# Loading the first expert tile's rows by a transfer of its own in a four-stage transformer kernel

## The chip, the cores and the metric

The kernel runs on one core of one Trainium2 chip. The metric is the device time of one execution in microseconds (us), start to end, as the median of the runs. A lower number is better.

## What is computed

Two transformer-like layers work on 2048 tokens (8 sequences of 256) with 256 features. Each layer normalises its input, and adds an attention part and a feed-forward part to it. The change lies in the feed-forward part of the first layer, a mixture of eight experts of which each token uses two, beside a shared expert:

```python
def _mlp(x, gw, uw, dw):
    return jax.nn.silu(x @ gw.T) * (x @ uw.T) @ dw.T
...
topk_idx, topk_w = _route(x2d, router_weight, e_score_correction_bias)
cw = jnp.zeros((T, E), jnp.float32).at[jnp.arange(T)[:, None], topk_idx].add(topk_w)

def expert_body(acc, ws):
    gw, uw, dw, cwe = ws
    y = _mlp(x2d, gw, uw, dw)
    return (acc + cwe[:, None] * y, None)
...
out = routed.reshape(orig_shape) + _mlp(x, shared_gate_w, shared_up_w, shared_down_w)
```

The attention of the first layer is a delta-rule recurrence of 16 heads, the second layer has a test-time-training attention and a second mixture of experts. The change touches none of these three.

## The kernel before

**Order of the stages.** The engines (PE for matmuls, DVE, ACT, POOL, and SP, which issues nearly all transfers) each run a hand-written program; semaphores tie them together. First come the layer norm, the routing and the shared expert, then 39 tiles of the routed experts, then the first attention in a loop over heads, then the second layer.

**The routed experts.** Token rows are sorted by expert through memory. The DRAM tensor `slot_rows` has 39 tiles of 128 rows, each row 256 features, one routing weight and padding, 272 numbers or 1088 bytes in all. SP first fills it with zeros (line 476), counted on the semaphore `e_zero`, which POOL awaits (line 2690) before its own sends. POOL then scatters the tokens' rows into it with 32 indirect transfers (`send`, line 2687), counted on `e_first` and `e_second`. SP waits for all of these (lines 519 and 520), and then loads the tiles back in groups of TG = 3 with `load_tiles` (line 510 on, the transfer on line 513) into `xs`, which has XBUF = 3 group buffers, each with a semaphore of its own, `e_x[g]`. The first three groups are loaded at once, one transfer behind the other; each of the ten later ones is loaded when the group three before it is used up. `store_tiles` (line 515) writes the results of a group to `slot_out`, from where POOL gathers them.

**What PE does per tile.** For each tile `n` the loop at lines 786 to 800 calls, in this order, `turn_x(n)` (line 731: two transposes, line 738), a load of the tile's expert number into a register of PE's sequencer (line 789), `expert_up` of the tile before (line 746), `turn_h` of the tile before that (line 755) and `expert_down` of the tile three back (line 765). `turn_x(n)` waits for `e_x` of its group where `n` is the first of a group. ACT copies each turned tile out (line 1475). Directly before the tiles PE runs the shared expert's last down projection (`shared_down`, line 708), and it then waits for the expert numbers and weights (lines 728 and 729).

The wait and the load, as they stand:

```python
if j % TG == 0:
    pe.wait_ge(e_x[g % XBUF], 16 * (g // XBUF + 1))
```

Of the kernel before, what the change touches and what calls it, by code (L numbers as in the profile page):

```python
# [16 lines left out]
P = 128  # L17
# [24 lines left out]
TG, XBUF, YBUF, GBUF = 3, 3, 2, 3  # L42
# [41 lines left out]
def build(nc, a, out):  # L84
    with ExitStack() as ctx:
# [3 lines left out]
        def sem(name):  # L89
            return ctx.enter_context(nc.semaphore(name))  # L90
# [59 lines left out]
        rt = sem("small_steps")  # L150
        moe_w, e_w = sem("shared_weights"), sem("expert_weights")
        m_gate, m_up, m_silu, m_h, m_down, m_added = (sem("shared_" + n) for n in "gate up silu h down added".split())
        e_zero, e_slots, e_ids, e_first, e_sent, e_second = (sem("e_" + n) for n in "zeroed slots tile_experts first_sent first_weights_gone second_sent".split())
        e_x = [sem(f"e_rows{g}") for g in range(XBUF)]
        e_xt, e_xk, e_gu, e_sg, e_h, e_ht, e_hk, e_dn, e_y = (sem("e_" + n) for n in "x_turned x_kept gate_up silu h h_turned h_kept down y".split())
        e_stored = [sem(f"e_stored{g}") for g in range(YBUF)]
# [7 lines left out]
        def esb(name, shape, dt=F32):  # L164
            return ectx.enter_context(nc.sbuf_tensor(name, shape, dt))
# [25 lines left out]
        xs = esb("xs", [P, XBUF, TG, ROW])  # L191
# [7 lines left out]
        slot_rows = nc.dram_tensor("slot_rows", (TILES0 * P, ROW), F32, kind="Internal").ap()  # L199
# [4 lines left out]
        def asb(name, shape, dt=F32):  # L204
            return actx.enter_context(nc.sbuf_tensor(name, shape, dt))
# [42 lines left out]
        slots = asb("slots", [P, NT, TOP0], mybir.dt.int32)  # L248
# [209 lines left out]
        def _(sp):  # L458
# [51 lines left out]
            def load_tiles(g):  # L510
                if g >= XBUF:
                    sp.wait_ge(e_y, TG * (g - XBUF + 1))
                sp.dma_start(xs[:, g % XBUF], slot_rows[g * TG * P:(g + 1) * TG * P].rearrange("(t p) n -> p t n", p=P)).then_inc(e_x[g % XBUF], 16)

            def store_tiles(g):
                sp.wait_ge(e_y, TG * (g + 1))
# [4 lines left out]
            for g in range(XBUF):  # L521
                load_tiles(g)
            for g in range(GROUPS):
                store_tiles(g)
                if g + XBUF < GROUPS:
                    load_tiles(g + XBUF)
# [53 lines left out]
        def _(pe):  # L580
# [149 lines left out]

            def turn_x(j):
                g = j // TG
                if j % TG == 0:
                    pe.wait_ge(e_x[g % XBUF], 16 * (g // XBUF + 1))
                if j >= 2:
                    pe.wait_ge(e_xk, j - 1)
                for kk in range(KD):
                    last = pe.transpose(bank[1 - j % 2][:, kk * P:(kk + 1) * P], xs[:, g % XBUF, j % TG, kk * P:(kk + 1) * P], ident[:])
                last.then_inc(e_xt, 1)
# [46 lines left out]
            for n in range(TILES0 + 3):  # L786
                if n < TILES0:
                    turn_x(n)
                    experts[n] = pe.value_load(tile_e[0:1, n:n + 1], min_val=0, max_val=E0 - 1)
                if 0 <= n - 1 < TILES0:  # L790
                    expert_up(n - 1, experts[n - 1])
                if n in (TILES0 - 1, TILES0):
                    for kk in range(KD):
                        project(first_unit, QRY if n < TILES0 else KEY, kk)
                if 0 <= n - 2 < TILES0:
                    turn_h(n - 2)
                if 0 <= n - 3:
                    expert_down(n - 3, experts.pop(n - 3))
# [2236 lines left out]
```

## Time and profile before

| | us |
|---|---|
| median of 3 runs | 1740.82 |
| lowest and highest run | 1740.14, 1742.18 |
| the profiled execution | 1741.03 |
| its span | 1739.2 |

The span is what the trace covers, from the first to the last instruction; 1.8 us of the profiled execution lie around it. All times in the rows are counted from the start of the span. "Idle before" is how long an engine did nothing ahead of an instruction, with the instruction or transfer that ended it. PEld is PE's weight load, and SPq, POOLq and PEldq are the sequencers of those engines. PEclk is the granted clock of PE as a share of full speed.

### The profile page before, as it was taken

What the parts mean: (1) busy time and instruction counts of PE and PEld (TensorE: products, weight loads), DVE (VectorE), ACT (ScalarE), POOL (GpSimd) and SP (SyncE); (2) the same over time, 40 slices, a digit from 0 to 9 for tenths busy, and PEclk for the clock granted to TensorE, in tenths of its full rate; (3) what the DMA queues carried; (4) which work ended last, traced back from release to release, by engine and by line L of the source; (5) the groups of instructions that cost most, each with busy time, mean ns of one, the idle gap of its engine ahead of it and who ended that gap; (6) DMA issues with size and microseconds to landing.
All of it is one profiled execution on the core that took longest, in us unless ns stands there. A gap on an engine that the chain in (4) does not pass through costs nothing.

```text
span 1739.2 us, 41709 instructions
## 1 busy us (share of the span) xinstructions
PE 1663.8 (96%) x14092; PEld 1226.2 (71%) x14092; DVE 1466.3 (84%) x3682; ACT 1203.6 (69%) x2912; POOL 1101.9 (63%) x1149
## 2 busy tenths in 40 slices
PE   8999899999999999999999999999987689999989
PEld 5577567777777777777777777777765566777677
DVE  6322599999999999999999999999996699999963
ACT  3034477777777777777777777777763488888863
POOL 1700067777777777776666666666666578888851
PEclk9999999999999999999999999999998699999999
DMA  9433310111110101100101000001002000000023
GB/s 316 165 107 105 98 32 23 38 32 27 31 36 21 40 21 37 30 24 25 27 15 30 15 27 24 18 24 27 15 9 61 1 1 2 1 2 2 1 77 107
DMA packets 66098, 73.85 MB, mean 42 GB/s; under 512 B 10975, under 2 KB 54767, under 8 KB 65775
## 3 DMA queue, kind: packets, MB, share of 16 engines
q1 hardware_dynamic: 62919, 63.92, 12.7%
q0 software_dynamic: 3072, 8.65, 1.5%
q8 instruction: 49, 0.80, 0.2%
q14 instruction: 58, 0.48, 0.1%
HBM read 55.45 MB, written 17.10 MB: 42 GB/s over the span
## 4 chain that ended last, share of the span: by engine, by line
PE 81%; DVE 8%; ACT 4%; POOL 3%; issue 2%; DMA 1%; SPq 0%; DVEq 0%; POOLq 0%
PE banks L781 20%; PE banks L940 7%; PE banks L808 4%; PE banks L895 3%; PE banks L816 3%; PE banks L914 3%; PE banks L824 3%; PE banks L746 3%; PE banks L853 3%; PE banks L861 3%; PE banks L867 2%; PE banks L1075 2%; PE banks L860 2%; PE banks L996 2%; PE banks L765 2%
## 5 line engine op out<-in xcount | busy, mean ns | idle before, releaser
L781 PE MATMUL banks<-xnT,hw 128*128 128x512 f32 x768 | 414.4, 623 | 2.5 <-DVE cv L2094 2.5
L2150 DVE CAST_PREDICATED MM<-lmask,banks 128x512 bf16<-128x512 uint32 x384 | 272.8, 710 | 38.6 <-PE banks L861 34.5
L2094 DVE SCALAR_TENSOR_TENSOR cv<-banks,hc,cv 128x510 f32<-128x510 f32 (+2 forms) x384 | 285.2, 743 | 5.5 <-ACT cv L1495 0.8
L1559 ACT ACTIVATE T<-banks 128x256 bf16<-128x256 f32 x384 | 149.3, 389 | 154.8 <-PE banks L853 153.7
L2761 POOL TENSOR_TENSOR X<-X,yrow 128x512 f32<-128x512 f32 x128 | 163.2, 1276 | 68.0 <-ACT yrow L1591 68.0
L2725 POOL TENSOR_TENSOR kn<-nsum,half_pos 128x4 f32<-128x4 f32 x64 | 65.5, 1023 | 143.4 <-DVE nsum L2119 143.4
L861 PEld LDWEIGHTS banks<-MM,T 128*128 128x128 bf16 x1536 | 103.9, 98 | 64.3 <-issue 47.4
L860 PEld LDWEIGHTS banks<-T,MM 128*128 128x128 bf16 x1280 | 98.8, 97 | 66.3 <-ACT T L1559 64.7
L2094 DVE SCALAR_TENSOR_TENSOR cv<-banks,hcv,cv 128x510 f32<-128x510 f32 (+2 forms) x192 | 141.5, 737 | 1.4 <-ACT cv L1495 1.3
L853 PEld LDWEIGHTS banks<-MM,Gb 128*128 128x128 bf16 x1536 | 83.9, 98 | 82.8 <-issue 43.0
L940 PE MATMUL banks<-ho,OT 128*128 128x256 f32 x512 | 142.2, 401 | 0.0
L1591 ACT ACTIVATE yrow<-banks,oinv 128x256 f32<-128x256 f32 x256 | 107.1, 473 | 45.9 <-POOL oinv L2756 45.4
L861 PE MATMUL banks<-MM,T 128*128 128x64 bf16 x1536 | 136.2, 193 | 0.5 <-ACT T L1559 0.5
L1499 ACT ACTIVATE raw<-cv 128x512 f32<-128x512 f32 x192 | 121.9, 635 | 4.6 <-DVE cv L2094 4.0
L860 PE MATMUL banks<-T,MM 128*128 128x64 bf16 x1280 | 118.4, 193 | 3.6 <-ACT T L1559 3.3
L781 PEld LDWEIGHTS banks<-xnT,hw 128*128 128x128 f32 x768 | 117.1, 192 | 6.5 <-DVE cv L2094 3.2
L853 PE MATMUL banks<-MM,Gb 128*128 128x64 bf16 x1536 | 109.2, 194 | 3.8 <-DVE MM L2150 3.8
L2155 DVE TENSOR_TENSOR Rb<-Rm,banks 128x256 bf16<-128x256 f32 x256 | 106.8, 417 | 6.3 <-POOL Rm L2752 5.6
L2756 POOL TENSOR_TENSOR oinv<-orr,half_neg 128x4 f32<-128x4 f32 x64 | 65.7, 1027 | 51.9 <-ACT orr L1569 51.7
L940 PEld LDWEIGHTS banks<-ho,OT 128*128 128x128 f32 x512 | 87.8, 191 | 6.8
L867 PE MATMUL banks<-Rb,MM 128*128 128x128 bf16 x640 | 88.3, 220 | 3.3 <-DVE Rb L2155 2.4
L1495 ACT ACTIVATE cv<-banks,hc 128x512 f32<-128x512 f32 x128 | 87.9, 687 | 2.9 <-PE banks L781 2.9
(319 smaller groups left out, 4833.0 us busy)
## 6 DMA issues: line engine op xcount, KB each, us to landing
MM<-in_eye SPq DMA_DIRECT2D x64, 256.0 KB, 2.7
slot_rows<-zeros SPq DMA_DIRECT2D x1, 5304.0 KB, 20.9
xs<-slot_rows SPq DMA_DIRECT2D x13, 408.0 KB, 3.9
slot_out<-ye SPq DMA_DIRECT2D x13, 384.0 KB, 2.7
hw<-in_hw SPq DMA_DIRECT2D x16, 256.0 KB, 3.5
wT<-in_winit SPq DMA_DIRECT2D x8, 384.0 KB, 4.3
wgu<-in_wgu SPq DMA_DIRECT2D x1, 2816.0 KB
w1c<-in_ew SPq DMA_DIRECT2D x16, 176.0 KB
```

Source lines behind the costliest of these rows:

```text
L781: ins = pe.matmul(PROJ[t][:], hw[:, kk, t, :], xnT[:, kk, u.b * BLK:(u.b + 1) * BLK], start=(kk == 0), stop=(kk == KD - 1))
L853: last = pe.matmul(o[:, k * 64:(k + 1) * 64], Gb[:, par, k, :], strips(MM[:, u.b, 0, k, :], size, 0, 1), start=True, stop=True)
L860: pe.matmul(o[:, k * 64:(k + 1) * 64], MM[:, u.b, 1, k, :], strips(T1[:, k, :], size, 0, 1), start=True, stop=True)
L861: last = pe.matmul(o[:, (TILES + k) * 64:(TILES + k + 1) * 64], T1[:, k, :], strips(MM[:, u.b, 1, k, :], size, 1, 1), start=True, stop=True)
L867: last = pe.matmul(solve_bank(u)[:, s * P:(s + 1) * P], MM[:, u.b, 1, s * NC + c, :], rhs[:, s, :], start=True, stop=True)
L940: last = pe.matmul(bank[7 - s][:, c * D:(c + 1) * D], OT[:, s * NC + c, :], ho[:], start=True, stop=True)
L1499: act.activation(raw[:, u.b % 2, t, :], cv[:, t, :], ACT.Silu).then_inc(act_silu, 1)
L1559: act.activation(strips(T1[:].rearrange("p i t -> p (i t)"), LEVELS[lv], 0, 1), grams_bank(u)[:, 0:TILES * 64].rearrange("p (k e) -> p k e ...
L1591: last = act.activation(yrow[:, s, c], bank[7 - s][:, c * D:(c + 1) * D], ACT.Copy, scale=oinv[:, u.b % 2, s * NC + c:s * NC + c + 1])
L2094: dve.scalar_tensor_tensor(o, y, taps_of(t)[:, TAPS - 1 - i:TAPS - i], o, ALU.mult, ALU.add).then_inc(dve_conv, 1)
L2150: dve.copy_predicated(dst, m, ps).then_inc(dve_mm, 1)
L2761: pool.tensor_tensor(xs, xs, yrow[:, s], ALU.add).then_inc(pool_x, 1)
```

## The change

The first group is loaded by two transfers in place of one: tile 0 alone, and right behind it tiles 1 and 2. The first counts on `e_zero`, which stands at 16 by then and goes to 32; the second on `e_x[0]`, as the whole group did. PE's `turn_x(0)` waits for `e_zero` at 32, and `turn_x(1)` waits for `e_x[0]`, where it had no such wait. The semaphore's name in the source is changed too.

```diff
             def load_tiles(g):
                 if g >= XBUF:
                     sp.wait_ge(e_y, TG * (g - XBUF + 1))
-                sp.dma_start(xs[:, g % XBUF], slot_rows[g * TG * P:(g + 1) * TG * P].rearrange("(t p) n -> p t n", p=P)).then_inc(e_x[g % XBUF], 16)
+                alone = 1 if g == 0 else 0
+                if alone:
+                    sp.dma_start(xs[:, 0, 0], slot_rows[0:P]).then_inc(e_zero, 16)
+                sp.dma_start(xs[:, g % XBUF, alone:], slot_rows[(g * TG + alone) * P:(g + 1) * TG * P].rearrange("(t p) n -> p t n", p=P)).then_inc(e_x[g % XBUF], 16)
...
             def turn_x(j):
                 g = j // TG
-                if j % TG == 0:
+                if j == 0:
+                    pe.wait_ge(e_zero, 2 * 16)
+                elif j % TG == 0 or j == 1:
                     pe.wait_ge(e_x[g % XBUF], 16 * (g // XBUF + 1))
```

## Rows read from the trace of the kernel before

**Rows 1.** The page: busy time of the engines and the chain's shares.
```profile
PE 1663.8 (96%) x14092; PEld 1226.2 (71%) x14092; DVE 1466.3 (84%) x3682; ACT 1203.6 (69%) x2912; POOL 1101.9 (63%) x1149
...
PE 81%; DVE 8%; ACT 4%; POOL 3%; issue 2%; DMA 1%; SPq 0%; DVEq 0%; POOLq 0%
```

**Rows 2.** The chain that ended last, 87.9 to 93.2: start, us, what.
```profile
85.57 2.42 DMA slot_rows<-xnr,slots
...
88.07 3.25 DMA xs<-slot_rows
91.31 0.14 issue
91.45 0.41 PE banks L738 x2
91.86 0.51 issue
92.36 0.43 PE banks L738 x2
```

**Rows 3.** The timeline, 84 to 96: start, us, engine, line, operation.
```profile
83.63 7.09 PE L708 MATMUL banks<-wsd,hT 96*128 96x256 f32 x32
...
88.07 1.44 SPq L513 DMA_DIRECT2D xs<-slot_rows  x3
...
91.42 0.20 PEld L738 LDWEIGHTS banks<-ident,xs 128*128 128x128 f32 x2 [1.10 <-issue]
91.45 0.41 PE L738 MATMUL banks<-ident,xs 128*128 128x128 f32 x2 [0.73 <-DMA xs<-slot_rows]
91.90 0.38 ACT L1475 ACTIVATE xT<-banks 128x256 f32<-128x256 f32 x1 [12.65 <-PE banks L738]
92.36 0.20 PEld L738 LDWEIGHTS banks<-ident,xs 128*128 128x128 f32 x2 [0.74 <-issue]
...
93.16 1.45 PE L746 MATMUL banks<-wgu,xT 128*128 x4 [0.36 <-issue]
```

**Rows 4.** Line 513, first transfer (88 to 88.3): issue and landing.
```profile
L513 SPq DMA_DIRECT2D xs<-slot_rows x1: 382/382/382, 88.1 to 88.1; - x1
...
DMA to landing us min/median/max: 3.2/3.2/3.2
```

**Rows 5.** Packets begun in 89.0 to 89.9, then in 90.4 to 91.0.
```profile
DMA packets 127, 0.14 MB, mean 154 GB/s; under 512 B 0, under 2 KB 127, under 8 KB 127
...
DMA packets 232, 0.24 MB, mean 392 GB/s; under 512 B 16, under 2 KB 232, under 8 KB 232
```

**Rows 6.** Line 506, the attention's 128 KB loads: issue and landing.
```profile
L506 SPq DMA_DIRECT2D ho<-in_ho x15: 342/343/343, 298.2 to 1273.3; - x15
...
DMA to landing us min/median/max: 1.9/2.1/2.1
```

**Rows 7.** Lines 734 and 789, PE's sequencer, 90 to 94: min/median/max ns, starts.
```profile
L734 PEldq EVENT_SEMAPHORE  x1: 51/51/51, 91.3 to 91.3; - x1
...
L789 PEldq TENSOR_LOAD <-tile_e x3: 306/316/497, 91.5 to 93.3; - x3
L789 PEldq FUSED_REGOPS  x3: 151/156/165, 92.0 to 93.7; - x3
L789 PEldq SEQ_ASSERT  x3: 18/18/28, 92.3 to 93.9; - x3
```

**Rows 8.** Line 513, second and third transfer (88.9 to 89.3): issue and landing.
```profile
L513 SPq DMA_DIRECT2D xs<-slot_rows x2: 488/489/490, 88.5 to 89.0; - x2
...
DMA to landing us min/median/max: 3.9/4.4/4.8
```

**Rows 9.** Busy us in the tiles' stage: PE, PEld, DVE, ACT, POOL, clock, DMA.
```profile
93.20:184.00 90.80, 90.80 (x436) 67.00 (x437) 24.34 (x73) 38.29 (x110) 0.00 (x0) 1.00 0.32 95
```

**Rows 10.** Transposes of tiles 3, 4 and 6 in PE's timeline.
```profile
96.06 0.38 PE L738 MATMUL banks<-ident,xs 128*128 128x128 f32 x2
98.73 0.38 PE L738 MATMUL banks<-ident,xs 128*128 128x128 f32 x2
...
103.71 0.38 PE L738 MATMUL banks<-ident,xs 128*128 128x128 f32 x2
```

**Rows 11.** Busy us and granted clock (third number from the end), two later stretches.
```profile
212.00:214.00 2.00, 2.00 (x14) 1.58 (x13) 1.29 (x3) 0.25 (x1) 0.00 (x0) 0.60 0.01 4
...
1360.00:1380.00 20.00, 16.13 (x97) 13.73 (x98) 13.13 (x50) 9.38 (x21) 13.26 (x6) 0.51 0.00 1
```

**Rows 12.** The same matmuls (line 816), 213 to 215.2, then 230 to 232.
```profile
L816 PE MATMUL banks<-raw x4: 634/634/773, 213.2 to 214.6; 128*128 128x256 f32 x4
...
L816 PE MATMUL banks<-raw x4: 379/379/435, 230.3 to 231.0; 128*128 128x256 f32 x4
```

More of the change, by code:

```diff
@@ L152, in build @@
         m_gate, m_up, m_silu, m_h, m_down, m_added = (sem("shared_" + n) for n in "gate up silu h down added".split())
-        e_zero, e_slots, e_ids, e_first, e_sent, e_second = (sem("e_" + n) for n in "zeroed slots tile_experts first_sent first_weights_gone second_sent".split())
+        e_zero, e_slots, e_ids, e_first, e_sent, e_second = (sem("e_" + n) for n in "zeroed_and_first_rows slots tile_experts first_sent first_weights_gone second_sent".split())
         e_x = [sem(f"e_rows{g}") for g in range(XBUF)]
```

## The prediction, made before the changed kernel was run

> **What bounds the kernel now.** I read the page first. PE is busy 96% of the span, and the chain that ended last lies on PE for 81% of it [rows 1]. So an edit helps only where it takes idle time from PE. The two loads and the one wait that change all act at one place, the step from the shared expert to the tiles. The chain at that place shows what to look for: POOL's last scatter lands, SP issues the load of three tiles at 88.07, and it takes 3.25 us to land, at 91.31; PE's first transposes start at 91.45 [rows 2]. The timeline shows the other side of that wait: PE works on line 708 until 83.63 + 7.09 = 90.72, and is then idle for 0.73 us [rows 3]. So this wait is short because most of the 3.25 us already lie beside PE's work. 0.73 us is all that an earlier tile 0 can give directly. It is 0.04% of the time.
>
> [...]
>
> **The second transfer and its wait.** SP's queue takes one more issue. An issue takes 382 to 490 ns [rows 4, 8], so the second transfer goes at 88.07 + 0.38 to 0.49 = 88.45 to 88.56. Together the two move the same 384 rows, and the stream is already running, so the data is there when the old group's data was, and the landing at 91.31 is the lower bound. The upper bound is the old second load: it was issued at about the same time and landed 3.9 us after it [rows 8], at about 92.5, but behind 768 rows and not 384. Between these I take 91.45, near the lower one, because the row count is the lower one's. Tile 1's transposes need this landing and the sequencer. The sequencer now passes tile 0's wait at about 90.35 and needs what it needed before, 92.36 - 91.31 = 1.05 us [rows 2], to reach tile 1: 91.4. The expert number is thus loaded beside line 708, if nothing else holds it. The new wait adds an instruction of 51 ns [rows 7] and about 0.1 us to the start of the transposes, 91.31 to 91.42 as before [rows 2, 3]. So tile 1 starts at about 91.55 in place of 92.36, **0.8 us** earlier. What follows on the sequencer, a further expert number and then line 746 at 93.16 [rows 3], keeps its distance of 0.80 us. ACT's copy of tile 0, 0.38 us from 91.90 [rows 3], moves forward with the transposes by 0.73 and is done at 91.55, before line 746 asks for it at about 92.35.
>
> The bounds of this term: with the second landing at 91.31 tile 1 starts at 91.42, a gain of 0.94. With it at 92.5, tile 1 starts at 92.6 and the term is a loss of 0.25.
>
> **The rest of the queue.** The loads of groups 1 and 2 are issued one issue later, at most 0.49 us. Group 1 landed at about 92.5 and group 2 at 89.0 + 4.8 = 93.8 [rows 8]. Their first tiles, 3 and 6, are transposed at 96.06 and 103.71 [rows 10]. So 3.5 and 9.9 us cover the delay, and even with PE 0.8 us earlier it costs nothing; without that cover it would be at most 0.49 us. SP's next work, the first store, waits for three finished tiles. POOL waits for `e_zero` at 16 only, long before the load, and has nothing behind the edit. DVE and ACT issue nothing more.
>
> **The sum.** Profiled execution 1741.03 - 0.8 = 1740.2 us. It stands 0.2 us above the median of the runs shown, so the forecast is **1740.0 us**, 0.05% less. About 0.2%, or 3.5 us, is what a measurement of this kernel can tell from no change, and the three runs alone differ by 2.0 us. So this is "no change that can be told", with a small gain inside it.
>
> [...] The second and third load landed 1.2 to 1.3 us behind the load before each, though each is 3.2 us by itself when nothing is ahead [rows 4, 8], so the fixed part of a transfer lies beside the data of the one before. [...]
>
> **Rivals.**
>
> *The fixed part is paid twice in a row.* If the second transfer only moved when the first had landed, it would land at 90.3 plus between 2.1 us [rows 6] and 3.2 us [rows 4], the lengths of a load of a third and of three thirds; I take 2.8, so 93.1. Tile 1 would start at 93.2, 0.85 us later than now, and the time would be **1741.7 us**, slower in sign. It decides from a landing later than 92.25. For it: nothing here shows a transfer of 384 rows that is cut in two. Against it: the spacing of the three loads [rows 8].
>
> *The second landing takes the gain back.* Between the two, a landing of 91.9 to 92.3 leaves tile 0 early and tile 1 where it was: about **1740.7 us**. For it: the stream starts slowly, with only 127 packets in its first 0.8 us [rows 5], and two sets of counts are now to be written.
>
> *The gain does not come out at the end.* PE could be earlier by 0.8 us through the tiles and then meet something in the first attention that does not move. DVE, at 84% [rows 1], paces the start of that stage in part. But its work hangs on PE's and ACT's there, so it should move too. The time would be **1740.8 us**.
>
> [...]
>
> *The change does nothing at its place.* PE's wait might end with another count than thought. The semaphore has 16 from the zeros, landed before the scatters, and reaches 32 by the load alone, so I see no way for that.
>
> **How the numbers follow.** Forecast, a gain of 0.6 to 0.95 us: 0.55. Second landing takes it back: 0.14. Fixed part twice: 0.07. Gain does not come out: 0.12. Clock, in either direction: 0.12, of which 0.05 is slower by over 0.2%, 0.04 faster by over 0.2%, and the rest between. All other cases are within 0.2%, so same is 0.91 from the cases. I move 0.01 to faster and 0.01 to slower for what no row shows: 0.05, 0.89, 0.06. For the range I take the terms' bounds, a gain of 0.95 and a loss of 0.85 us, from the median: 1739.9 to 1741.7. To that I add the scatter of runs and the smaller moves of the clock: 1738.2 to 1742.2.
>
> **What would show it.** Tile 0's load lands at 90.2 to 90.6. The idle time before the first line 738 falls from 0.73 to under 0.1 us, with the shared expert named before it and no DMA. Tile 1's transposes start near 91.55, and line 746 near 92.35 in place of 93.16. Tile 1's wait should be for the second transfer, landed near 91.45. PE has no idle time after that until the last tile. I am wrong if the first line 746 is not at least 0.5 us earlier, if tile 1's transposes wait for a landing after 92.2, or if the total moves by more than 3.5 us with the granted clock as before.

## The result, and the profile after

| | before | after |
|---|---|---|
| median of 20 runs, us | 1740.99 | 1738.51 |
| lowest and highest, us | 1739.69, 1743.10 | 1736.70, 1739.94 |
| profiled execution, us | 1741.03 | 1738.59 |
| its span, us | 1739.2 | 1736.8 |

The ratio is 0.9984, with a 95% interval of 0.9978 to 0.9990. That is 2.5 us less, or 0.16%: inside 0.2%, inside the range, and three times the 0.8 us that the steps of the prediction gave. The interval lies clear of 1, so 20 runs of each do tell the change, which the prediction had as one that can't be told. All medians and ratios here and below are over fast runs; one slow run, of the kernel "timed before" further on, took 2109 us at a mean clock of 0.75 and is left out. Where the other 1.7 us come from is the question of the experiments.

The page of the kernel after, the same lines as [rows 1]:

```profile
PE 1661.8 (96%) x14092; PEld 1223.9 (70%) x14092; DVE 1466.0 (84%) x3682; ACT 1202.0 (69%) x2912; POOL 1101.6 (63%) x1149
```

The timeline of the kernel after at the step into the tiles answers to [rows 3]. Its lines are numbered otherwise: the down projection is line 711, the transposes 743, the first expert product 751. The two transfers are 515 and 516.

```profile
83.67 7.73 PE L711 MATMUL banks<-wsd,hT 128*128 128x256 f32 x35
...
88.76 0.33 SPq L515 DMA_DIRECT2D xs<-slot_rows  x1
...
91.25 0.38 PE L743 MATMUL banks<-ident,xs 128*128 128x128 f32 x2
...
92.67 0.44 PE L743 MATMUL banks<-ident,xs 128*128 128x128 f32 x2 [1.04 <-DMA xs<-slot_rows]
...
93.43 1.45 PE L751 MATMUL banks<-wgu,xT 128*128 x4 [0.33 <-issue]
```

Tile 0 follows the down projection, which ends at 91.40, with no idle time. The wait has moved to tile 1: 1.04 us for the second transfer. In this execution everything from the early part on is 0.69 us later than in the trace of before, so I count from the end of the down projection: the first expert product starts 93.43 - 91.40 = 2.03 us after it, against 93.16 - 90.72 = 2.44 [rows 3]. The step is **0.41 us** shorter, half of the forecast, and under the 0.5 us that the prediction had named as the least if it was to be right.

The chain of the kernel after gives the second transfer's time, against one transfer of 3.25 in [rows 2]:

```profile
88.76 0.33 SPq L515
89.09 0.04 issue
89.13 3.49 DMA xs<-slot_rows
```

The first transfer, line 515 of the kernel after:

```profile
L515 SPq DMA_DIRECT2D xs<-slot_rows x1: 331/331/331, 88.8 to 88.8; - x1
...
DMA to landing us min/median/max: 2.2/2.2/2.2
```

So tile 0 lands 2.2 us after its issue, as forecast, and the rest of the group at 92.62, 3.86 us after the first issue. That is 0.6 us more than the undivided load took.

Then I compared the starts of the same matmuls (the n-th of 14092) in the two traces. The difference, after less before:

| at, us | 67 | 124 | 173 | 224 | 1273 | 1658 | 1736 |
|---|---|---|---|---|---|---|---|
| difference, us | +0.69 | +0.27 | +0.27 | -1.27 | -1.54 | -1.26 | -2.45 |

From 67 to 124 lies the step: -0.42. Nothing changes in the tiles. Then -1.54 come at once between 173 and 224, and -1.19 behind 1658. Both are places where before has 3.4 us at the lower level of the clock, a granted clock of 0.50, that after has not: the mean over 211 to 217 is 0.72 against 1.00, and over 1658 to 1680 it is 0.84 against 0.92. It does not cost as much everywhere: between 1273 and 1658 before has 3.4 us more of it too (41 against 37), and there the difference moves 0.28 us the other way. The stretch 212 to 214 had a granted clock of 0.60 in [rows 11]; in the kernel after:

```profile
212.00:214.00 2.00, 2.00 (x20) 1.57 (x16) 1.69 (x3) 0.38 (x1) 0.00 (x0) 1.00 0.02 4
```

PE's work ahead of that place is the same in both: from 192 to 212 it stands idle seven times, for 0.41, 0.60, 1.00, 1.30, 0.57, 0.65 and 0.93 us in before, and for the same lengths within 0.01 us in after. Only in before does the lower level follow. So in this pair of traces the clock gives most of the difference. Is that chance, or does the change cause it?

### The profile page after: what moved, and what is told of

It is laid out like the page before. It is cut to its first block, busy times and chain, and to the rows that moved or that the text cites. A ratio compares the mean times of both kernels' runs of the same rounds, so it can differ in the third digit from the quotient of the medians.

```text
span 1736.8 us, 41710 instructions
## 1 busy us (share of the span) xinstructions
PE 1661.8 (96%) x14092; PEld 1223.9 (70%) x14092; DVE 1466.0 (84%) x3682; ACT 1202.0 (69%) x2912; POOL 1101.6 (63%) x1149
## 4 chain that ended last, share of the span: by engine, by line
PE 81%; DVE 8%; ACT 4%; POOL 3%; issue 2%; DMA 1%; SPq 0%; DVEq 0%; POOLq 0%
PE banks L786 20%; PE banks L945 7%; PE banks L813 4%; PE banks L900 3%; PE banks L919 3%; PE banks L821 3%; PE banks L829 3%; PE banks L858 3%; PE banks L751 3%; PE banks L866 3%; PE banks L872 2%; PE banks L1080 2%; PE banks L865 2%; PE banks L1001 2%; PE banks L770 2%
## 5 line engine op out<-in xcount | busy, mean ns | idle before, releaser
L2757 POOL TENSOR_TENSOR Rm<-bv,Wu 128x256 f32<-128x256 f32 x64 | 43.7, 683 | 72.9 <-ACT Wu L1578 70.4
```

## The experiments

### The two kernels once more, and two variants

Theory A: falls of the clock come and go from run to run, and the change gives its 0.4 us. Theory B: the change itself does away with the fall near 212. The first two kernels are the two of the comparison, unchanged. The third keeps both transfers but takes the early start away:

```diff
                 if j == 0:
                     pe.wait_ge(e_zero, 2 * 16)
+                    pe.wait_ge(e_x[0], 16)
```

The fourth loads tile 1 alone too, counted on a semaphore that has stood at 32 since the start:

```diff
-                alone = 1 if g == 0 else 0
+                alone = 2 if g == 0 else 0
                 if alone:
                     sp.dma_start(xs[:, 0, 0], slot_rows[0:P]).then_inc(e_zero, 16)
+                    sp.dma_start(xs[:, 0, 1], slot_rows[P:2 * P]).then_inc(moe_w, 16)
...
-                elif j % TG == 0 or j == 1:
+                elif j == 1:
+                    pe.wait_ge(moe_w, 3 * 16)
+                elif j % TG == 0 or j == 2:
```

> The kernel before, unchanged. The two traces so far differ by 2.4 us, of which the step into the tiles gives only 0.4; 1.5 us come at 212 to 216, where the trace of before has 3.4 us at the lower clock and the trace of after has none. Theory A (the fall at 212 comes and goes from run to run): this trace may lack it, and the time is still about 1741. Theory B (before always has it, after never): it is there again. Either way line 746 starts for the first time near 93.2.

> The kernel after, unchanged. Theory A: the fall of the clock at 212 may be there, and the ratio is still near 0.9985. Theory B: no fall at 212 again. The second transfer lands 3.4 to 3.6 us after its issue and PE idles about 1.0 us for it.

> Both transfers of the change, but tile 0 also waits for the second one. If the split itself costs what the trace of after shows (second landing 3.9 us after the first issue, against 3.25 for the undivided load), tile 0 starts 0.6 us later than in the kernel before and the time is 0.6 us above before and 1.0 us above after. The rival, that the gain comes from the clock or from the placement of the program and not from the early tile, expects about the time of after, 2.4 us under before.

> Tiles 0, 1 and 2 each by a transfer of its own, each awaited by its own transposes. If tile 1's start hangs on the landing of the second transfer, a transfer of 128 rows in its place lands about 0.5 us sooner, the idle time before tile 1 falls from 1.0 to about 0.5 us, and the time is 0.5 us under after. The rival, that each further transfer costs some 0.6 us before the next can land, expects no gain at tile 1 and a third transfer too late for tile 2, with about the time of after or 0.3 us more.

Measured, as ratios to the kernel before on the same chip (1756.07 us): before again 0.9996 (0.9987 to 1.0005), after again 1.0000 (0.9991 to 1.0009), split without the early start 1.0001 (0.9992 to 1.0010), each alone 0.9997 (0.9988 to 1.0006). No kernel can be told from the kernel before, and all are about 15 us slower than before was in the first comparison. The expectations about the step could not be tested: PE came to it too late. The timeline of "before again" shows PE in the shared expert (the tile loads are issued at 89 here too):

```profile
70.71 1.88 PE L644 MATMUL banks<-xnT,wsg 128*128 128x512 f32 x4
73.68 0.59 PE L654 MATMUL banks<-xnT,wsu 128*128 128x512 f32 x1 [1.09 <-issue]
75.08 0.59 PE L654 MATMUL banks<-xnT,wsu 128*128 128x512 f32 x1 [0.81 <-issue]
77.17 0.59 PE L654 MATMUL banks<-xnT,wsu 128*128 128x512 f32 x1 [1.51 <-issue]
79.28 1.01 PE L654 MATMUL banks<-xnT,wsu 128*128 128x512 f32 x1 [1.51 <-issue]
...
98.00 10.55 PE L708 MATMUL banks<-wsd,hT 128*128 128x256 f32 x48
108.39 0.60 PE L738 MATMUL banks<-ident,xs 128*128 128x128 f32 x4
109.34 1.45 PE L746 MATMUL banks<-wgu,xT 128*128 x4 [0.35 <-ACT xT L1475]
```

One matmul at a time, with gaps that wait for nothing the profile shows. The down projection ends at 108.55, the three loads had landed by about 95, and the first expert product starts 0.79 us after it. It is 0.78 to 0.79 in all four traces. There is no wait for the change to shorten.

### A second time, on another chip

The same four kernels, on a chip on which PE might not be held up.

> The kernel before, unchanged, a further time: in the last four runs PE was held up for 16 us in the shared expert (issue gaps between 72 and 92) in kernels of either kind, so that it came to the tiles 17 us after the loads had landed, and nothing of the change could show. If PE is not held up here, its wait for the first load is there again, 0.7 us, line 746 starts 2.44 us after the shared expert's end, and the time is near 1741. The fall of the clock near 212 is open: Theory A has it in some executions of either kernel, Theory B in every execution of this one and none of the changed one.

> The kernel after, unchanged. Where PE is not held up, line 746 (751 here) starts 2.03 us after the shared expert's end, 0.4 us less than before. My theory: the time is 0.4 us under before and what the first comparison has beyond that, 2.0 us, comes and goes with the clock. The rival: the ratio of the first comparison, 0.9984, repeats, 2.5 us less, and the fall near 212 is missing again.

> Both transfers, with tile 0 waiting for the second as well. By the trace of after the second lands 0.6 us later than the undivided load, so PE idles 0.7 + 0.6 = 1.3 us before tile 0, line 746 starts 3.05 us after the shared expert's end in place of 2.44, and the time is 0.6 us over before if nothing else changes. The rival, by which the gain lies in the placement of the program or in the clock and not in the early tile, expects this kernel 2.5 us under before like the kernel after.

> Tiles 0, 1 and 2 each by its own transfer. If tile 1 waits for the second landing, it starts about 0.5 us sooner than in the kernel after, line 746 starts 1.5 us after the shared expert's end in place of 2.03, and the time is 0.5 us under after. The rival, that a further transfer costs as much as it saves, expects 2.0 us there and a wait of tile 2 for the third transfer.

PE was held up here as well, and the step was 0.78 to 0.79 us in all four. Ratios to 1756.35 us: before 0.9996 (0.9987 to 1.0006), after 1.0000 (0.9991 to 1.0009), split without the early start 1.0005 (0.9996 to 1.0014), each alone 1.0002 (0.9993 to 1.0011).

These two comparisons still say something. Over both, 22 executions of the kernel after have a mean 0.2 us above that of 88 of the kernel before, with a 95% interval of about 0.6 us either way. So where the first load is hidden, the change is worth nothing. The 2.5 us of the first comparison then do not come from where the program lies or from one instruction more by themselves. They were seen only with the wait.

And theory B fell as it was put. The fall of the clock behind the tiles (212 in the first trace, about 228 here) is in the traces of "before" both times, but also in the first of "after", in the first of the split and in both of "each alone"; it is missing in the second of "after" and the second of the split. PE's steps were equal in all of these. A weaker form of it stays open: over the first pair, these and the timed kernels of the next section, the fall is in all four traces of the kernel before and in one of the four of the kernel after, and in five of the six of the other two. Here, with the load hidden, any such leaning is worth under a microsecond, since the times are equal within 0.6 us about a difference of 0.2.

### The step made again on purpose

To have the wait back on a chip that holds PE up, SP was made to issue the first load by PE's progress: after the second of the last down projection's four parts.

```diff
             sp.wait_ge(e_second, 16 * NT)
+            sp.wait_ge(m_down, 2 * NBLK - 1)
```

This one line was added to all four kernels.

> The kernel before with one more wait of SP ahead of the first tile load: for the middle of the shared expert's last down projection. That issues the load about 2.5 us before the end of line 708, as in the first trace (2.65 us), whether PE was held up earlier or not. Both theories expect the step of the first trace: landing 3.25 us after the issue, PE idle for about 0.8 us, line 746 about 2.5 us after the end of line 708.

> The kernel after with the same wait of SP. My theory: tile 0 lands 2.2 us after its issue and starts without idle time, the second transfer lands 3.4 to 3.6 us after its own issue, PE idles about 1.1 us for it before tile 1, and the gated-up matmul (line 751) starts 2.1 us after the end of the down projection, 0.4 us sooner than in the timed before. The time is 0.4 us under it, too little for the timing alone to tell. The rival, that the change by itself gives 2.5 us, expects a time 2.5 us under the timed before.

> The same wait of SP, both transfers, and tile 0 waiting for the second as well. If the split delays the landing of the group by 0.6 us, tile 0 starts 0.6 us later than in the timed before and line 751 starts about 3.1 us after the down projection. If the split costs nothing, as my prediction took it (0.14 us), it is 2.65 us.

> The same wait of SP, and tiles 0, 1 and 2 each by its own transfer and with its own wait. If the second landing sets tile 1, a second transfer of 128 rows in place of 256 lands about 0.5 us sooner, and line 751 starts 1.6 us after the down projection. The rival, that every further transfer costs as much as it saves, expects 2.1 us, as in the timed after, and a wait of tile 2 for the third transfer.

The step was there again. PE's timeline, timed before:

```profile
106.78 3.62 PE L709 MATMUL banks<-wsd,hT 128*128 128x256 f32 x16
111.24 0.41 PE L739 MATMUL banks<-ident,xs 128*128 128x128 f32 x2 [0.84 <-DMA xs<-slot_rows]
112.12 0.43 PE L739 MATMUL banks<-ident,xs 128*128 128x128 f32 x2 [0.48 <-issue]
112.91 1.45 PE L747 MATMUL banks<-wgu,xT 128*128 x4 [0.36 <-issue]
```

Timed after:

```profile
106.81 1.03 PE L712 MATMUL banks<-wsd,hT 128*128 128x256 f32 x4
107.68 0.38 PE L744 MATMUL banks<-ident,xs 128*128 128x128 f32 x2
108.82 0.44 PE L744 MATMUL banks<-ident,xs 128*128 128x128 f32 x2 [0.76 <-DMA xs<-slot_rows]
109.59 1.45 PE L752 MATMUL banks<-wgu,xT 128*128 x4 [0.33 <-issue]
```

Timed split without the early start (its down projection ends at 106.50):

```profile
107.46 0.41 PE L745 MATMUL banks<-ident,xs 128*128 128x128 f32 x2 [0.96 <-DMA xs<-slot_rows]
108.34 0.43 PE L745 MATMUL banks<-ident,xs 128*128 128x128 f32 x2 [0.47 <-issue]
109.12 2.05 PE L753 MATMUL banks<-wgu,xT 128*128 x4 [0.36 <-issue]
110.97 0.63 PE L745 MATMUL banks<-ident,xs 128*128 128x128 f32 x2
111.39 2.27 PE L753 MATMUL banks<-wgu,xT 128*128 x4
```

Timed each alone:

```profile
106.82 0.81 PE L713 MATMUL banks<-wsd,hT 128*128 128x256 f32 x3
107.47 0.38 PE L747 MATMUL banks<-ident,xs 128*128 128x128 f32 x2
108.27 0.43 PE L747 MATMUL banks<-ident,xs 128*128 128x128 f32 x2 [0.42 <-DMA xs<-slot_rows]
109.06 1.45 PE L755 MATMUL banks<-wgu,xT 128*128 x4 [0.35 <-issue]
```

| | end of down projection to first expert product, us | whole group landed after first issue, us | median of 11 runs, us | ratio to before on the chip (1756.07) |
|---|---|---|---|---|
| timed before | 2.51 | 3.19 | 1757.8 | 1.0009 (1.0000 to 1.0018) |
| timed after | 1.75 | 3.43 | 1755.4 | 0.9993 (0.9984 to 1.0002) |
| timed, no early start | 2.63 | 3.32 | 1758.6 | 1.0011 (1.0002 to 1.0020) |
| timed, each alone | 1.43 | 3.15 | 1755.2 | 0.9993 (0.9984 to 1.0002) |

The step is 0.76 us shorter with the change, so the forecast's 0.8 holds here. The split by itself costs 0.12 (the group lands 0.13 us later; 0.24 in the timed after, and not later at all with three transfers), not the 0.6 that I had read from the one trace of after: the second transfer took 3.06 and 2.95 us here, counted from its own issue, and 3.49 there. The 2.63 us of the split without the early start are the 2.65 that follow from the prediction's own 0.14 us; the 3.1 that I expected from the one trace did not come. Tile 1 by a transfer of its own takes another 0.32 off. The timed after was expected at 2.1 us, but its second landing was sooner than in the trace of after; "each alone" was expected at 1.6. The third transfer is in time: PE has no wait for a transfer after tile 1. The times of the last two kernels with an early start, 1755.4 and 1755.2, can't be told apart.

But the rival of the timed after had a point too: it expected 2.5 us, I expected 0.4, and it is 2.3. Taking the two kernels with a late tile 0 together and the two with an early one (22 executions each), the means differ by 2.9 us, with a 95% interval of 2.1 to 3.6. Their steps differ by (2.51 + 2.63) / 2 - (1.75 + 1.43) / 2 = 0.98 us. As in the first comparison, some 2 us are left over: a step read from one trace per kernel, with landings that spread by half a microsecond, does not cover them.

**Where they may be.** The trace of the timed split without the early start shows one place. The eight expert products of tiles 0 and 1 take 2.05 and 2.27 us in fours, against 1.45 and 1.35 in the timed after. The stretches of its trace (granted clock third from the end):

```profile
106.00:109.00 3.00, 1.33 (x7) 0.49 (x5) 0.69 (x1) 0.58 (x2) 0.00 (x0) 1.00 1.00 339
109.00:110.00 1.00, 0.88 (x3) 0.67 (x4) 0.00 (x0) 0.19 (x1) 0.00 (x0) 0.91 0.10 34
110.00:113.00 3.00, 3.00 (x8) 1.80 (x7) 0.34 (x1) 0.70 (x2) 0.00 (x0) 0.50 0.00 0
113.00:116.00 3.00, 3.00 (x16) 2.10 (x15) 1.00 (x4) 1.02 (x3) 0.00 (x0) 0.96 0.02 5
```

PE stood idle three times for 0.96, 0.47 and 0.36 us, and then, from 109.8, its clock was at the lower level, 0.50, for 3.4 us, in the middle of the tiles, where PE was busy all of the time (3.00 of 3.00 us in 110 to 113). This cost 1.51 us: the first expert product starts at 109.12 here and 109.59 in the timed after, 0.47 earlier, and at 141 the same matmul is 1.04 later. The timed before had 0.84, 0.48 and 0.36 us of idle time and no fall at the step in the one execution that was traced. Its fall lies behind the tiles, at the place of the first trace's fall at 212:

```profile
113.00:116.00 3.00, 3.00 (x14) 1.99 (x14) 0.34 (x1) 0.80 (x3) 0.00 (x0) 1.00 0.02 6
...
231.70:235.00 3.30, 3.30 (x16) 2.49 (x16) 1.99 (x7) 0.28 (x1) 0.00 (x0) 0.50 0.01 2
```

The timed after has none there, and between 224 and 232 of its trace the timed before falls back against it by 1.54 us, as in the first pair. But the timed "each alone", which is as early, has the fall too, and so has the split without the early start. Single traces differ in other places as well: 2.4 us between the timed before and the timed after had come in their first 7 us.

Every run has its mean granted clock. Over the 22 runs each it is 0.9810 with a late tile 0 and 0.9819 with an early one, a difference of 0.00095 with a standard error of 0.0003. With the lower level at 0.50 that is 2 x 0.00095 x 1755 = 3.3 us more at it per execution. What it is worth depends on where it lies. At 1.51 us for 3.4 us, as above, it would be 1.5 us, and with the step 0.98 + 1.5 = 2.5, inside the 2.1 to 3.6 that were measured. But the runs themselves give a lower price. Within each set of 22, a run with a mean clock lower by 0.001 is 0.66 us longer (standard error 0.15), and 0.48 us (0.11) within the 88 runs of the eight kernels before. By these the 0.00095 is worth 0.5 to 0.6 us, an estimate, and with the step 1.6; then 1.3 of the 2.9 us have no place.

So what is shown is this. The shorter wait gives its own 0.4 to 0.8 us. Some 2 us more come with it, and were seen only where the wait is there. The kernels with the late tile 0 have more time at the lower clock, and single stretches of it, at the step and behind the tiles, cost 1.5 us each. That the longer wait brings them about, and that they are the whole of the 2 us, is not shown. Of the first comparison the runs of before have a clock on record for the profiled one alone, 0.985, against a mean of 0.9874 over the 20 of after. That points the same way and does not prove it.

## Why the prediction was right, and where it was not

**The place and its parts held.** PE's wait for the first load was what the change moved. Tile 0's load was to land 2.2 us after its issue; it took 2.2, and 2.1 in the three timed kernels that have it. The idle time before tile 0 went from 0.73 to none. The sequencer began to load the first expert number while the down projection still ran, at 91.1 with an end at 91.40, and was done with it at about 92.0, ahead of the second landing at 92.62. In the timed "each alone", where the second transfer lands at 107.89, tile 1 starts only at 108.27, 1.02 us after tile 0's landing at 107.25: there the sequencer's 1.05 us, as the prediction had them, set the start. The later groups were covered: PE is busy for all of 93.43 to 184 in the kernel after.

**The second landing was mis-sized in the first trace.** The prediction took 91.45 for a second issue at about 88.5, so 2.95 us. It took 3.49, and the first expert product started 0.41 instead of 0.81 us earlier. The timed kernels gave 3.06 and 2.95. So the term was right at the size of the timed kernels, and the spread, half a microsecond on 3, is as large as the gain. The rival "the second landing takes the gain back" was half true in that one execution.

**The fixed part is not paid twice.** The prediction wrote that each of the three loads takes 3.2 us with nothing ahead of it, but its rows show that for the first alone; the fourth and fifth, issued singly at 104.81 and 112.28, took 3.7 and 3.9. Its argument, from landings 1.2 to 1.3 us apart, holds all the more. The group lands at most 0.6 us later by the split, and mostly 0.1 to 0.2, where the rival put it 1.8 us later and decided from 0.94. Cutting one load in two has at most a small price here, 0.12 us of the step, which is no more than landings differ from run to run (2.95 to 3.49 us for the same second transfer); the change as a whole made the step 0.76 us shorter in spite of it.

**What failed is the size of the sum.** It priced the idle time at the step at its own length only, and gave 0.8 us, a third of what was measured. In the first pair of traces most of the rest lies at later falls of the clock, to which the prediction gave a chance of 0.12, in either direction: 1.54 us at 212 and 1.19 us behind 1658, in time at the lower level that before has and after has not. The 0.05 and 0.04 of that chance stand for a clock that moves the time by over 0.2%, and no comparison here shows one; what was measured is 634 ns for a matmul of line 816 at 213 to 215.2, where the clock is low, against 379 at 230 to 232 [rows 12], and 1.51 us for one fall of 3.4 us in the tiles. The prediction did not have the idle stretches at the step themselves, after which the clock fell in one timed trace, at that cost of 1.51 us. How much of the 2 us is due to which, and whether all of it is the clock, stays open.

**What was luck.** The sign of the gain was right for a reason. That the total came out as forecast, under 0.2% and inside the range, was not: 0.8 and 2.5 both lie under 3.5 us, and 1738.51 is 0.3 us above the lower end of a range that was widened for scatter.

**"The gain does not come out at the end" fell.** The offset of 0.27 us between the traces is the same at 124 and at 173, and the timed kernels carry theirs unchanged from 141 to 189 us too.

## What to carry to other kernels

Shortening a short wait of PE in the middle of dense work can bring more than the wait's length: 2.5 us for a step of 0.4 here, and 2.9 for 0.98. Idle stretches of under a microsecond were followed by 3.4 us at a clock of 0.50 in one trace (0.96, 0.47 and 0.36 us) and not in another (0.84, 0.48 and 0.36), so read the granted clock in the stretch behind the wait, in more than one execution, and compare mean clocks over many runs before a difference is put down to it. Splitting off what is needed first cost 0.12 us in the timed kernels, with the two transfers issued 0.38 us apart, but the wait moved to the second part (1.04 us in the kernel after), so look there for what is left. And when a change sits on a wait of under a microsecond, find out whether the wait is there in every execution: where PE came to the tiles over 10 us after the loads had landed, the change was worth nothing (a difference of 0.2 us, give or take 0.6).

## What the runs showed of the hardware that was not expected

In all twelve traces of the experiments, of every kernel, PE was held up in the shared expert from about 71 to 92 us, and in neither of the first two: it was busy for 8.8 to 10.9 of these 21 us in the twelve, and for 20.1 and 20.6 in the two. In the trace of "before again" matmuls of 590 ns started 1.40 or 2.10 us apart, later ones 1.39 to 2.81 us, all of them multiples of about 0.70 us, and none of these gaps is put down to another engine or to a transfer. It began with the clock at its full level. The stretches of "before again":

```profile
60.00:72.00 12.00, 12.00 (x42) 7.30 (x40) 0.99 (x2) 1.19 (x2) 9.28 (x11) 1.00 0.30 107
72.00:80.00 8.00, 3.08 (x6) 0.85 (x4) 0.69 (x1) 0.00 (x0) 6.06 (x8) 0.86 0.29 104
80.00:92.00 12.00, 5.47 (x7) 1.84 (x7) 0.06 (x1) 0.00 (x0) 5.78 (x6) 0.50 0.38 127
```

The first row is the stretch before, with PE fully busy; in the second the gaps are there and the clock falls only near its end; in the third PE is busy for less than half of the time, at the lower level. The hold-up costs 16 us, more than six times what this change gives: the same matmul is 0.84 us later than in the first trace at 70 and 16.9 us later at 91. It is the reason why the same kernel takes 1741 us in one comparison and 1756 in the others. Its cause was not tried.
